# Weighed units of a mixture of experts: GpSimd's adds into the accumulator replaced by accumulating transfers

## The reference

```python
x = x + cross_attention(layernorm(x), ctx)              # ctx (16, 375, 256), one head
h = layernorm(x)
router_probs = softmax(h @ w_router)                    # 8 experts
gate_weights = softmax(h @ w_gating / 0.1)
g = einsum('bsh,ehf->ebsf', h, w_gate)                  # all 8 experts, F = 1024
u = einsum('bsh,ehf->ebsf', h, w_up)
expert_out = einsum('ebsf,efh->ebsh', silu(g) * u, w_down)
cw = router_probs * gate_weights
cw = cw / (sum(cw) + 1e-9)
x = x + einsum('ebsh,bse->bsh', expert_out, cw)
```

## Time and profile before

| | before |
|---|---|
| median of three runs | 964.14 us |
| profiled execution's span | 961.7 us |
| TensorE (PE) busy | 956.4 us, 99% |
| TensorE weight load (PEld) | 887.8 us, 92% |
| VectorE (DVE) | 744.5 us, 77% |
| ScalarE (ACT) | 483.2 us, 50% |
| GpSimd (POOL) | 797.4 us, 83% |
| transfers on SP's queue q1 | 54.91 MB, 19.6% of 16 engines |

### The profile page before, as it was taken

The page is one execution under the profiler, slowest core; times in us unless marked ns, Lnnn a source line. Parts: engine busy times, 40 slices in busy tenths (PEclk is TensorE's granted clock), DMA queues, the critical chain, the costliest instruction groups (busy, mean ns, idle before and its releaser), DMA issues.

```text
span 961.7 us, 14792 instructions
## 1 busy us (share of the span) xinstructions
PE 956.4 (99%) x5089; PEld 887.8 (92%) x5089; DVE 744.5 (77%) x1280; ACT 483.2 (50%) x855; POOL 797.4 (83%) x640
## 2 busy tenths in 40 slices
PE   9999999999999999999999999999999999999998
PEld 7999899999999999999999999999999999999998
DVE  4997557787877877788877787778877778777995
ACT  6987544454545444444544444445445454445442
POOL 5899976766888888888988888888898888888885
DMA  7472512311010110021100110011100200111135
GB/s 217 119 171 73 145 38 75 109 64 42 22 44 23 42 62 24 22 64 42 44 22 23 45 61 22 23 64 42 45 23 22 74 31 23 36 51 42 39 51 141
DMA packets 73232, 55.85 MB, mean 58 GB/s; under 512 B 30244, under 2 KB 69485, under 8 KB 73158
## 3 DMA queue, kind: packets, MB, share of 16 engines
q1 hardware_dynamic: 73150, 54.91, 19.6%
q10 hardware_dynamic: 8, 0.00, 0.0%
HBM read 46.58 MB, written 6.48 MB: 55 GB/s over the span
## 4 chain that ended last, share of the span: by engine, by line
PE 98%; DMA 1%; ACT 0%; DVE 0%; issue 0%; SPq 0%; DVEq 0%; ACTq 0%
PE ps L355 96%; PE ps L1878 1%; DMA xf<-in_L_xattn_Wk 1%; PE ps L1914 0%; PE ps L1866 0%; PE ps L1931 0%; DVE early L1350 0%; ACT arena L912 0%; PE ps L1957 0%; ACT xf L920 0%; ACT xf L912 0%; ACT early L899 0%; PE ps L1824 0%; DVE arena L366 0%; ACT arena L920 0%
## 5 line engine op out<-in xcount | busy, mean ns | idle before, releaser
L355 PE MATMUL ps<-arena 128*128 128x448 f32 (+5 forms) x2064 | 388.4, 339 | 0.2
L355 PEld LDWEIGHTS ps<-arena 128*128 128x128 f32 (+2 forms) x2064 | 343.6, 186 | 21.4 <-POOL arena L696 0.4
L702 POOL TENSOR_TENSOR arena<-shared,arena 128x448 fp32r<-128x448 f32 x196 | 252.3, 1301 | 120.6 <-ACT arena L1087 116.8
L355 PE MATMUL ps<-xc_hi,w_hi 128*128 128x448 f32 x904 | 330.6, 366 | 0.0
L355 PE MATMUL ps<-xc_hi,w_lo 128*128 128x448 f32 x904 | 330.2, 365 | 0.0
L355 PE MATMUL ps<-xc_lo,w_hi 128*128 128x448 f32 x904 | 330.2, 365 | 0.0
L355 PEld LDWEIGHTS ps<-xc_hi,w_lo 128*128 128x128 f32 x904 | 169.8, 188 | 13.6
L355 PEld LDWEIGHTS ps<-xc_hi,w_hi 128*128 128x128 f32 x904 | 169.8, 188 | 13.3
L355 PEld LDWEIGHTS ps<-xc_lo,w_hi 128*128 128x128 f32 x904 | 169.9, 188 | 13.2
L1080 ACT ACTIVATE shared<-shared 128x448 f32<-128x448 f32 x180 | 101.5, 580 | 145.5 <-DVE shared L1476 73.9
L819 POOL TENSOR_TENSOR xsacc<-xsacc,xf 128x448 f32<-128x448 f32 x104 | 119.3, 1158 | 0.0
(11 more groups left out here) (168 smaller groups left out, 1154.3 us busy)
## 6 DMA issues: line engine op xcount, KB each, us to landing
early<-in_L_ffn_w_down SPq DMA_DIRECT2D x16, 512.0 KB, 3.8
xf<-cw_dram SPq DMA_DIRECT2D x16, 448.0 KB, 4.7
shared<-in_ctx SPq DMA_DIRECT2D x16, 336.0 KB
w_raw<-in_L_ffn_w_gate SPq DMA_DIRECT2D x17, 256.0 KB, 2.8
w_raw<-in_L_ffn_w_up SPq DMA_DIRECT2D x17, 256.0 KB, 3.2
early<-in_L_ffn_w_gate SPq DMA_DIRECT2D x15, 256.0 KB, 2.9
early<-in_L_ffn_w_up SPq DMA_DIRECT2D x15, 256.0 KB, 3.1
xsacc<-in_x SPq DMA_DIRECT2D x8, 224.0 KB, 6.2
```

Source lines behind the costliest of these rows:

```text
L355: ins = nc.tensor.matmul(dst, w, m, start=first and i == 0, stop=last and i == len(passes) - 1, skip_group_check=onto)
L702: nc.gpsimd.tensor_tensor(h[:, 1, j, at:at + TC], tile, h[:, 0, j, at:at + TC].bitcast(fp32), ALU.subtract).then_inc(hid_lo_done, 1)
```

## The change

The add of `add_unit` becomes an accumulating transfer of the 128 x 448 float32 buffer (224 KB), issued on GpSimd's queue. The single count `unit_done` becomes two semaphores, one for even and one for odd units, each of which rises by 16 when a transfer has landed. `unit_there(engine, u)` waits for the transfer of unit u. VectorE's wait in `weigh` is now for the landing of the transfer of unit u - 2, GpSimd's own wait for that of the unit a pair of groups earlier with the same destination, and `turn` waits for the landing of the last one at its place. Nothing else moves.

```diff
-        unit_ready, weighed_done, unit_done = sem("unit_ready"), sem("weighed_done"), sem("unit_done")
+        unit_ready, weighed_done = sem("unit_ready"), sem("weighed_done")
+        unit_added = [sem("unit_added0"), sem("unit_added1")]
@@
+        def unit_there(engine, u):
+
+            first = UNITS * CP
+            if u >= first:
+                engine.wait_ge(unit_added[u % 2], DMA * ((u - first) // 2 + 1))
@@ add_unit
                 pool.wait_ge(weighed_done, u + 1)
 
-                at_least(pool, unit_done, u - 2 * UNITS * CP + 1)
-                to = unit_at(g, k)
-                nc.gpsimd.tensor_tensor(to, to, weighed[u % 2], ALU.add).then_inc(unit_done, 1)
+                unit_there(pool, u - UNITS * CP)
+                pool.dma_start(unit_at(g, k), weighed[u % 2], accum_op=ALU.add).then_inc(unit_added[u % 2], DMA)
@@ weigh
-                    at_least(ve, unit_done, u - 2 - UNITS * CP + 1)
+                    unit_there(ve, u - 2)
                     to = weighed[u % 2]
@@ turn
-                ve.wait_ge(unit_done, UNITS * (len(TURNED) - 2 * CP + cp) + k + 1)
+                unit_there(ve, UNITS * (len(TURNED) - CP + cp) + k)
                 to = unit_at(GROUPS - 2 * CP + cp, k)
```

## The result

The changed kernel takes 992.93 us (median of 992.17 to 994.39) against 964.83 us of the kernel before on the same chip: a ratio of 1.0302, 95% interval 1.0286 to 1.0318. The profiled execution's span went from 961.7 to 991.1 us, 29.4 us more. Some executions of these kernels, the one before included, took 977 to 979 us, and three took 1173 or 2452 us: the ratios and intervals leave these out, the medians of the experiments don't.

What follows compares the result with a forecast made beforehand. TensorE, busy 99% of the span, was taken as the bound; 26 stalls of 4.2 - 2.1 = 2.1 us add 54.6 us to the 961.7 us span, 1016.3, plus 2.5 us outside it: 1019 us, range 981 to 1085.

Steps and rivals of the forecast that it cites:

- TensorE bounds, GpSimd's relief is worth nothing: In the loop TensorE has no gap, so removing 119.3 us of adds from GpSimd gains nothing.
- One wait, in 26 places: VectorE's weigh(g, 2) waits for the landing of unit (g, 0) and delays TensorE in groups 4 to 29.
- The slack of 2.1 us: Time from issuing unit (g, 0) on GpSimd to its landing before weigh(g, 2) delays TensorE's gate product 4: 2.1 us.
- The price D: Time from issue to landing of one accumulating transfer: 4.2 us, between 2.9 and 6.7.
- The base of 2.8 us: Part of the landing time, taken from SyncE's 224 KB store: 2.8 us, between 2.3 and 3.4.
- The second read: The accumulating transfer also reads its destination, 448 KB in all, which lengthens the landing by 0.8 us.
- The low rival, a short transfer at 982 us: Second read and descriptor work overlap, landing takes about 2.8 us, each stall 0.7 us, 982 us; chance 0.17.
- The rule of the Trainium skill: GpSimd-issued transfer: about 2.0 us fixed plus bytes at 436 GB/s; 2.5 or 3.1 us, so 977 to 990 us.
- The issue on GpSimd: Issuing 104 transfers, each near the add's 1.16 us, changes nothing on GpSimd; 2.0 us to spare before TensorE needs low-part weights.
- The last turn, put at nothing: After the loop, the last turn has 4.35 us from the preceding add for its landing; cost put at nothing.
- L1513 shorter: VectorE's products of two SBUF tiles, 1157 ns, should get shorter without GpSimd's adds, with no effect on the time.
- the prediction's own upper end: Landing of 6.7 us, from a 4.7 us broadcast, 1.2 issue and 0.8 add: 26 stalls of 4.6 us, 1084 us.

Runs made afterwards that it cites:

- 78 transfers: The changed kernel with only units 1 to 3 of each group added by transfers, unit (g, 0) by GpSimd's arithmetic: 963.95 us, ratio 1.0003.
- the later weighing: The changed kernel with VectorE's weigh(g, 2) moved behind the sums of the up products, all 104 transfers kept: 965.41 us, ratio 1.0023.

## Why the prediction was right, and what was off

The range held the time (981 to 1085, 992.93), and so did the direction. Point by point:

- *TensorE bounds, GpSimd's relief is worth nothing.* Right. With 78 transfers and no stall, 963.95 against 963.42 us.
- *One wait, in 26 places.* Right: 26 waits of VectorE, 26 of TensorE, and unit (g, 0) alone gives the whole loss.
- *The slack of 2.1 us.* Right. Unchanged adds that end 1.1 us later cost 0.16 us in each group, as worked out from it.
- *The price D.* This is the term that was mis-sized: 4.2 us forecast, 3.2 measured. The base of 2.8 us came from a store into the chip's main memory, issued by SyncE; the same 224 KB from SBUF to SBUF, issued by GpSimd, land in 2.2 us, issue included. So base and issue together were 2.2 and not 3.4. The second read, put at 0.8, measured 1.0. By the measured D the sum is 26 x 1.1 = 28.6 us, against 28.1 in the trace. The forecast of 1019 lay twice as far from 964 as the result, and this term is the reason.
- *The low rival, a short transfer at 982 us,* lay nearer than the forecast, in landing time (2.8 against 3.2) as in the sum, and its chance of 0.17 was too small. The result is between the two. The rule of the Trainium skill (DMA: Bandwidth & Descriptors, section Anatomy of one DMA) gave, as an estimate, 2.5 us for the plain transfer and 3.1 with the second read; the traces have 2.2 and 3.2, and the 990 us that follow from it stand 3 us from the result. Its lower sum was added up wrongly in the prediction: with 2.5 us it is 26 x 0.4 = 10 us more, 975 and not 977.
- *The issue on GpSimd.* Right in effect: 1.04 us on the mean, near the add's 1.16, and no wait for the weights' low parts. GpSimd is not the bound.
- *The last turn, put at nothing.* Right for its reason (3.1 us of 4.35), but 1.3 us were lost behind the last stall, with the held product in the chain, which the prediction didn't have.
- *L1513 shorter.* Right: all 60 took 1155 ns at the median before and 734 after. The one exception is the held product at the end.
- *Large stalls.* The sum took each stall at its own length. Had D been 4.2 us, stalls of 2.1 us might have cost more than that through the clock, as 23 of 26 stalls of 2.4 us did. With stalls of 4.6 us, the prediction's own upper end, the high side of the range was probably too low.

## What to carry to other kernels

Before an add on an idle-enough engine is turned into a transfer, find who reuses its source buffer next and in which order that engine works: a landing of 3 us is free where the reuse is 5 us away and costs all that it exceeds the slack by in every round where something urgent is queued behind the wait. If a wait must become longer, move it behind what the bounding engine needs (here: one line, 29 us to 2 us), not only the work that it waits for. Price a transfer by a row with the same memories at both ends and the same issuer, if there is one: a store from SyncE was 0.6 us too dear here, and no run tells which of the two made the difference.

## What was not expected of the hardware

- Of 26 stalls of TensorE of about 2.4 us, 23 were followed by a granted clock of 0.50 for some 3 us, and so cost about 1.5 us more than their length; three of the same length were not, nor was any of 26 stalls of 1.1 us.
- An accumulating transfer of 224 KB landed after 3.2 us, a plain one after 2.2 us. The issue took 0.88 and 0.56 us of GpSimd at the median.
- Single landings took 5 to 7.4 us (the longest of 104 in the changed kernel 7.4). Off the path they cost nothing; ahead of a tight wait one cost about 1 us. The cause is open.
- A product of two SBUF tiles on VectorE took 3.93 us beside an unbroken series of GpSimd's instructions in the changed kernel, 4.29 us with the later weighing, and 0.81 us beside nearly the same series in the kernel before; alone it takes 0.62 us.
